# Mask phase of a four-phase transformer kernel: reordered statistics, pair eviction, row sums and low-part splits

## The reference, cut to what matters

```python
xq  = layer_norm(x, qn_w, qn_b)            # [16, 256, 512]
ctx = layer_norm(context, cn_w, cn_b)
q = (xq @ q_w).reshape(B, N, H, D)         # H = 16 heads of D = 32
kv = (ctx @ kv_w).reshape(B, M, 2, H, D)
k, v = kv[:, :, 0], kv[:, :, 1]
attn = einsum('bnhd,bmhd->bhnm', q, k) * scale
attn = where(xa_mask[:, None, :, :], neg, attn)
attn = softmax(attn, axis=-1)
out = einsum('bhnm,bmhd->bnhd', attn, v).reshape(B, N, C)
x = x + out @ proj_w + proj_b
...
```

## Time and profile before

| | |
|---|---|
| median of three runs | 2735.47 us |
| the profiled execution, its own time | 2735.95 us |
| its span, as the profile shows it | 2733.9 us |
| busy over the span | PE 96%, DVE 72%, ACT 57%, POOL 34% |
| granted TensorE clock, mean | 0.983 |

### The profile page before, as it was taken

How to read it: one execution, slowest core, us unless ns; L and a number is a source line. 1 busy time by engine, 2 the same in 40 slices (tenths; PEclk the granted TensorE clock), 3 DMA queues, 4 the chain that set the end, 5 groups by cost and what they waited for, 6 DMA issues and landing times.

```text
span 2733.9 us, 67256 instructions
## 1 busy us (share of the span) xinstructions
PE 2618.4 (96%) x23144; PEld 2244.9 (82%) x23144; DVE 1956.6 (72%) x5443; ACT 1565.1 (57%) x4742; POOL 923.0 (34%) x1097
## 2 busy tenths in 40 slices
PE   6899998998899999999999999999899999999997
PEld 5777777777688888888888888888788888888886
DVE  6888788787644344434458888888788888888887
ACT  5677767767511111111238777777667676776764
POOL 4656656655110000000002333333434343434332
PEclk8999999999999999999999999999999999999999
DMA  5666656655421101111321111111322221222210
GB/s 160 151 153 154 162 148 154 163 148 143 131 62 47 61 31 61 46 46 47 92 82 36 46 46 46 46 46 52 125 69 84 74 87 61 92 69 70 84 54 24
DMA packets 313622, 236.12 MB, mean 86 GB/s; under 512 B 150736, under 2 KB 240848, under 8 KB 312656
## 3 DMA queue, kind: packets, MB, share of 16 engines
q1 hardware_dynamic: 313552, 235.22, 30.2%
HBM read 137.65 MB, written 63.96 MB: 74 GB/s over the span
## 4 chain that ended last, share of the span: by engine, by line
PE 79%; DVE 8%; ACT 7%; issue 4%; DMA 1%; SPq 1%; POOL 0%; DVEq 0%; ACTq 0%; POOLq 0%
PE cross_work L181 16%; PE mlp_acc L3297 13%; PE mlp_f L3279 13%; PE causal_work L181 9%; PE mask_work L181 6%; PE cross_scores L2294 3%; ACT mask_prob_even L964 3%; PE cross_scores L2271 2%; PE cross_attended L2324 2%; PE causal_scores L2294 2%; PE causal_scores L2271 2%; DVE mask_scores L1555 2%; PE causal_attended L2324 1%; PE mask_scores L2271 1%; ACT mask_prob L964 1%
## 5 line engine op out<-in xcount | busy, mean ns | idle before, releaser
L3072 ACT ACTIVATE mlp_h<-mlp_f,mlp_b1col 128x512 f32<-128x512 f32 x128 | 88.3, 690 | 525.9 <-PE mlp_f L3279 525.9
L3279 PE MATMUL mlp_f<-mlp_xT_hi,mlp_w 128*128 128x512 f32 x1024 | 335.5, 389 | 0.9 <-DVE mlp_xT_lo L3165 0.9
L3179 DVE CAST mlp_hT_hi<-mlp_h 128x512 fp32r<-128x512 f32 x128 | 58.1, 454 | 370.0 <-ACT mlp_h L3072 369.8
L3297 PE MATMUL mlp_acc<-mlp_w,mlp_hT_hi 128*128 128x512 f32 x1024 | 315.2, 389 | 0.0
L964 ACT ACTIVATE cross_prob<-cross_scores,cross_low 128x256 f32<-128x256 f32 x512 | 237.5, 491 | 63.1 <-DVE cross_low L1549 63.1
L964 ACT ACTIVATE causal_prob<-causal_scores,causal_low 128x128 f32<-128x128 f32 (+1 forms) x512 | 210.6, 436 | 93.6 <-DVE causal_low L1555 93.6
L1555 DVE CUSTOM_DVE_ANT_0 mask_scores<-mask_scores,mask_mask 128x256 f32<-128x256 f32 x512 | 200.9, 454 | 47.8 <-PE mask_scores L2271 35.2
L3279 PEld LDWEIGHTS mlp_f<-mlp_xT_hi,mlp_w 128*128 128x128 f32 x1024 | 192.4, 188 | 42.0 <-DVE mlp_xT_lo L3165 1.3
L3297 PEld LDWEIGHTS mlp_acc<-mlp_w,mlp_hT_hi 128*128 128x128 f32 x1024 | 192.2, 188 | 40.0
L181 PE MATMUL causal_work<-causal_xT_hi,causal_w 128*128 128x256 f32 x1008 | 217.0, 293 | 0.3 <-DVE causal_qk_parts L1505 0.3
L3279 PE MATMUL mlp_f<-mlp_xT_lo,mlp_w 128*128 128x512 f32 x512 | 199.2, 389 | 0.0
(11 more groups left out here) (368 smaller groups left out, 8136.7 us busy)
## 6 DMA issues: line engine op xcount, KB each, us to landing
cross_x_in<-after_attention SPq DMA_DIRECT2D x17, 512.0 KB, 4.1
mask_x_in<-in_x SPq DMA_DIRECT2D x16, 512.0 KB, 4.4
mask_c_in<-in_ctx SPq DMA_DIRECT2D x16, 512.0 KB, 4.8
mask_res<-in_x SPq DMA_DIRECT2D x16, 512.0 KB, 3.8
after_attention<-mask_res SPq DMA_DIRECT2D x16, 512.0 KB, 3.1
mlp_x<-after_attention SPq DMA_DIRECT2D x8, 1024.0 KB, 5.5
mlp_stage<-in_L_xattn_fc_w SPq DMA_DIRECT2D x8, 1024.0 KB, 5.7
after_layer<-mlp_y SPq DMA_DIRECT2D x8, 1024.0 KB, 4.4
```

The source lines that it names most:

```text
L3072: act.activation(h32[:, m % 2, :], F1[m % 2][:], ACT.Gelu, bias=b1col[:, m:m + 1]).then_inc(s["gelu"], 1)
L3279: ins = pe.matmul(F1[m % 2][:], W[2 * (m // 4)][:, a, k, m % 4 * P:(m % 4 + 1) * P], xT[p][:, k, :], start=(k == 0 and n == 0), stop=(k == ...
L3297: ins = pe.matmul(ACC[t][:], hT[a][:, m % 2, t * P:(t + 1) * P], W[2 * (m // 4) + 1][:, p, m % 4, :], start=(m == 0 and n == 0), stop=(m = ...
```

## The change

Nothing is added and nothing is removed in the turns 1 to 15: every instruction is still there once, in another place of its engine's list. GpSimd's and SyncE's lists are unchanged.

```diff
@@ -1044,24 +1044,23 @@
 
             if cur and prev:
                 exps(b, 0)
+            if prev:
+                pair_kept(b, -1)
+            if not cur:
+                yield ROOM
+                post_hi(b, 1)
+                yield ROOM
+                return
+            if prev:
+                values(b, 0)
                 exps(b, 1)
-                values(b, 0)
-            if prev:
-                pair_kept(b, -1)
-            if cur and prev:
                 exps(b, 2)
+                qk(b, 1)
                 exps(b, 3)
-                qk(b, 1)
-            if cur:
-                high_halves(b, 0, 0)
-                high_halves(b, 0, 1)
-            if not cur:
-                yield ROOM
+            high_halves(b, 0, 0)
             if prev:
                 post_hi(b, 1)
-            if not cur:
-                yield ROOM
-                return
+            high_halves(b, 0, 1)
             if prev:
                 values(b, 1)
                 values_high(b)
@@ -1114,11 +1113,13 @@
             copy(b, 12)
             copy(b, 13)
             copy(b, 14)
-            post_hi(b + 1, 0)
             if not nxt:
+                post_hi(b + 1, 0)
                 yield ROOM
             copy(b, 15)
-            if not nxt:
+            if nxt:
+                post_hi(b + 1, 0)
+            else:
                 yield ROOM
 
         def causal_turn(b, prev, cur, nxt):
@@ -1730,7 +1731,8 @@
             minima(b, 2)
             if nxt and prev:
                 project(b, 0)
-            over_sums(b, 0)
+            else:
+                over_sums(b, 0)
             if not prev:
                 turn_over(b + 1, 0)
                 turn_over(b + 1, 1)
@@ -1757,6 +1760,11 @@
             if not nxt:
                 yield ROOM
                 project(b, 1)
+            if nxt and prev:
+                qk_lo(b + 1, 0)
+                mask_floats(b + 1)
+                if after:
+                    front(b + 2)
             normed(b, 0)
             if nxt and not prev:
                 turned(b + 1, 2)
@@ -1764,15 +1772,14 @@
             over_sums(b, 1)
             if not prev:
                 matrix_lo(3)
-            if nxt:
+            if nxt and not prev:
                 qk_lo(b + 1, 0)
                 mask_floats(b + 1)
-            else:
-                yield ROOM
-                yield ROOM
-            if nxt and after:
                 front(b + 2)
-            elif nxt:
+            elif not nxt:
+                yield ROOM
+                yield ROOM
+            if nxt and not after:
                 yield ROOM
 
                 dve.sem_inc(s["chain"], 2)
@@ -2468,9 +2475,11 @@
                 pe.wait_ge(s["qk_lo"], KC * b + 1)
                 queries(b, 1)
                 keys(b, 1)
+            pe.wait_ge(s["v_ready"], 2 * b + 1)
+            values(b, 1, 0)
+            if prev:
                 turn_sums(b, -1)
-            pe.wait_ge(s["v_ready"], 2 * b + 1)
-            values(b, 1, None if prev else 0)
+                values(b, 1, 1)
 
             scores(b, 1)
             pe.wait_ge(s["qk_lo"], KC * b + 2)
@@ -2507,7 +2516,8 @@
                 project(b, 1, 0)
                 if nxt:
                     project(b, 1, 1)
-            turn_sums(b, 0)
+            if not (nxt and prev):
+                turn_sums(b, 0)
 
             if not nxt:
                 yield ROOM
```

More of the change, by code:

```diff
@@ L1046, in mask_turn @@
                 exps(b, 0)
-                exps(b, 1)
-                values(b, 0)
             if prev:
                 pair_kept(b, -1)
-            if cur and prev:
-                exps(b, 2)
-                exps(b, 3)
-                qk(b, 1)
-            if cur:
-                high_halves(b, 0, 0)
-                high_halves(b, 0, 1)
             if not cur:
                 yield ROOM
+                post_hi(b, 1)
[3 more added lines that the diff above has]
+                values(b, 0)
+                exps(b, 1)
+                exps(b, 2)
+                qk(b, 1)
+                exps(b, 3)
+            high_halves(b, 0, 0)
             if prev:
                 post_hi(b, 1)
-            if not cur:
-                yield ROOM
-                return
+            high_halves(b, 0, 1)
             if prev:
@@ L1766, in mask_turn @@
                 matrix_lo(3)
-            if nxt:
+            if nxt and not prev:
                 qk_lo(b + 1, 0)
                 mask_floats(b + 1)
-            else:
+                front(b + 2)
+            elif not nxt:
                 yield ROOM
                 yield ROOM
-            if nxt and after:
-                front(b + 2)
-            elif nxt:
+            if nxt and not after:
                 yield ROOM
```

## The result

The changed kernel takes 2694.68 us, the median of four runs (2689.70 to 2697.07), against 2735.02 us for before (four runs, 2732.65 to 2736.23). The ratio is 0.9851, 95% interval 0.9834 to 0.9868: 40.3 us faster, where 55.8 were forecast. The profiled execution is the fastest of the four, 2689.70 us.

A forecast was written before the change was run, and what follows sets the result against it. TensorE's mask-phase waits, mainly on ScalarE's eviction, were the target: 36.66 + 0.25 + 0.1 + 0.2 + 0.2 - 0.3 = 37.1 us a turn against 40.94. Over 14 turns 53.8, plus 2.3: 2680, range 2663 to 2708.

The forecast's parts named there:

- blocked copies: Rival: two `over_sums` and `post_lo` on VectorE each wait for a GpSimd instruction, 1.9 us a turn on top, 2706; chance 0.20.
- a floor of 36.36: Turn without TensorE waits: 36.66 us by one form, less 0.3, half of the 0.57 by which the other form is lower.
- 0.75 of new waits: Per turn: 0.25 before `scores(b, 3)`, 0.1 for `attend` on `normed`, 0.2 on ScalarE's copies, 0.2 for the VectorE-GpSimd port.
- The long stalls and the clock: Chunks 0 and 2: waits of 2.10 and 0.94 us before row sums, plus 1.58 us of half clock in ten turns.
- Row sums behind the keys: Chunks 2 and 3: scores follow the projection at once; 0.25 us of the 0.94 wait left, 0.56 us of work moves.
- Statistics: VectorE, behind chunk 3's minima: next minima 1.75 us after `scores(b+1, 0)`, not 3.45; `attend` waiting on `normed` costs 0 to 0.1.
- Chunk 0 and ScalarE's chain: Chunk 0's 2.10 us wait goes; ScalarE's copies end 18.45 us after `scores(b, 0)`, TensorE arrives at 18.4: 0.2 us wait.
- The port, 0.2 us: VectorE's `over_sums` beside GpSimd's work: a blocked one waits at most 1.13 us, both 0 to 2.3 a turn; 0.2 taken.
- Turn 15: Has the same stall as the other turns, 2.56 us, of which 2.3 us was counted as gained.
- the floor's time of 2666: Rival: both engines' arrivals fit and nothing is blocked, 36.1 us a turn, 70 us gained, 2666; chance 0.14.
- The slower case: Rival: `attend(b+1, -2, 2)` waits for `normed` behind statistics waiting for rows of turn b+2; 2741 at 4.6 us late; chance 0.05.

The follow-up runs named there:

- the kernel before with the reduction: Kernel before, with the lift (constant added to a head's two minima) as a TENSOR_REDUCE over pairs, nothing else: 2724.38 us.
- The two remedies: Changed kernel with the lift as a TENSOR_REDUCE, 2680.70 us; or with chunk 3's queries and keys evicted one head earlier, 2680.48; both together 2667.39.
- the kernel whose TensorE shows no wait: Changed kernel with the lift as a TENSOR_REDUCE, chunk 3's queries and keys evicted one head earlier, head 0's lift directly behind its minima: 2662.14 us.
- without any lift: Constant not added to the minima in chunks 0 and 2, its instruction left out: changed kernel 2659.79 us, kernel before 2703.06 us.
- The form with 128x1: Changed kernel with the constant added by two TENSOR_SCALARs of one element per partition in place of one of two elements: 2684.56 us.

## Why the prediction was right, and where it was not

The time lies in the range and the direction is right. But 2695 is nearer to "blocked copies", 2706, than to the forecast's 2680, and the range reaches that far only for this rival, whose copies cost nothing that can be seen here: that much was luck. The 37.97 us a turn lie above the 36.5 to 37.6 that were to show the forecast. And two errors of opposite sign stand inside its 37.1 us. The forecast was a floor of 36.36 (36.66 less 0.3) and 0.75 of new waits. Measured are a floor of 35.71 and 37.97 - 35.71 = 2.26 above it.

*The long stalls and the clock:* right in that both go. The 2.10 and the 0.94 before the row sums are gone, and with them the half clock of the earlier trace rows in turns 2 to 14. But the half clock had cost far less than the 1.58 us counted for it. Chunks 0 and 1 of the kernel before, in a turn with it and in one without:

```profile
282.64:295.75 13.11, 11.01 (x122) 0.87 0.41 145
295.75:304.25 8.50, 8.50 (x78) 1.00 0.98 204
323.35:334.87 11.52, 9.42 (x121) 1.00 0.38 136
334.87:344.68 9.81, 8.99 (x77) 1.00 0.98 207
```

Together they take 21.61 us with it and 21.33 without: what chunk 0 lost, chunk 1 did not have to wait. In the kernel before with the reduction the two kinds of turn take 40.45 and 40.17 us, the same difference of 0.28. The turns of the second form were the longer ones because the lift was held in them, in chunk 2 (11.62 us, against 10.60).

*Row sums behind the keys, "0.25 us of the 0.94 as left":* this is the step that failed. 0.89 is left in nine of the turns and 0.42 in the others, plus 0.43 before the projection in the nine. I named the four `turned` on VectorE as what is late; the rows show VectorE idle for 0.62 us ahead of the low part, and ScalarE late. Its list from the minima of chunk 2 to the eviction was not laid out; only that of chunk 0 was. The two remedies bear it out from both ends. The eviction stands 8.88 us behind the chunk's scores in the long turn; with an earlier start of the exponentials (the reduction) it is 7.62, with one head fewer in front 7.98. The chunk's 1.45 us over its 8.99 without waits is the largest part of the 2.64 by which a long turn exceeds the floor.

*The floor:* busy time of a turn that stalls is not its time without stalls. By the rows, busy falls from 36.66 to 36.47, 36.11 and 35.71 as the waits go, though the work is the same. What that 0.95 us consists of was not tested; a group's row may cover short waits between its matmuls.

*Statistics:* right. The next minima start 1.96 us after `scores(b+1, 0)` (forecast 1.75, before 3.45), and `attend` waits for `normed` by 0.2 us at most in two turns. It also waits for the DMA transposes, by up to 0.36 us (and by 1.43 in turn 1, as before the change); 1.1 us of slack was forecast there, and it was less.

*Chunk 0 and ScalarE's chain:* right to a few tenths. Chunks 0 and 1 take 18.7 us in the long turn and 18.32 in the short one, forecast 18.6; 0.25 us of wait stands before the turning of chunk 1's probabilities, where I had put 0.2 one step later, before `scores(b, 2)`.

*The port, 0.2 us:* the mechanism was right, the place wrong. The copy in `over_sums` is held in the long turns (1.22 us) and `post_lo` more than before, its mean rises from 1050 to 1467 ns, and both are absorbed as far as can be seen: in the kernel whose TensorE shows no wait, that copy still takes 0.83 us and `post_lo` 1.19 to 1.41. One such copy had been held before the change too, for 1.34 us in turn 0. What cost time is the lift, which I had not looked at, since its usual row reads 0.17 us. The Trainium skill, page "SBUF — State Buffer", section "Who interferes with whom", says that a tensor_scalar in a two-port mode and an operation with two SBUF inputs share a lock with GpSimd, while tensor_reduce on this chip never contends. The trace agrees on all three: 1.44 us for the two-element TENSOR_SCALAR, 1.80 for `post_lo`, and at most 0.16 for the TENSOR_REDUCE.

*Turn 15:* 2.3 us forecast, 2.8 measured up to its last scores. The 2.56 stall is gone, but 3.08 stands in its chunk 1, where 2.28 stood.

*The rivals:* the floor's time of 2666 is what the changed kernel reaches once the lift and the eviction are mended. "Blocked copies" had the kind of hold right, and at 2706 was too slow, because the copies it named are covered. The slower case did not arise: VectorE never waited for the rows of turn b+2.

Why 40 and not 56? Not because of the hold alone: it was there before, and the change is worth 43.7 us with it gone from both kernels, 43.3 without any lift. With the lift a turn goes from 40.94 to 37.97, 2.97 us against the 3.84 forecast. In the terms of the sum, TensorE is busy 510.91 / 14 = 36.49 us a turn, 0.13 more than the 36.36, and idle for 1.48 in place of 0.75. Of the 1.48, 0.97 are the two waits in chunk 2 (9.8 and 3.8 us over 14 turns), for which 0.25 was put in; that is most of what is missing. ScalarE's chain there is as long as before: in a turn with a held lift the eviction of queries and keys stands 8.88 us behind the chunk's scores, and in the kernel before it stood 8.89 behind them (scores at 344.68 in the earlier trace rows):

```profile
353.57 0.60 ACT L942 ACTIVATE mask_qk_parts<-mask_work 128x512 fp32r<-128x512 f32 x1
```

There the wait for the pair, which is gone, had covered it. The kernel with the row sums' part alone shows the same wait of 0.42 or 0.88 us by itself.

Open is why the hold begins in four turns before and in nine after. GpSimd's last gain ends 0.30 us after the lift is issued in the long turn and 0.27 in the short one, where the lift ends with that gain. Each part alone also has it (7, 14 and 8 turns). Each count is of one execution, and how it varies between executions of one kernel was not measured.

## What to carry to other kernels

Where a loop's turns come in two forms, split each form by stage before averaging them; the second form of before already held one of the terms that decided here. When a stall goes, lay out the chain of every engine between the same two points, not only of the one that was reordered. Read the longest and not only the median time of small instructions ahead of a chain: one that usually takes 0.17 us took 1.44, and writing it as a reduction and issuing it one head sooner, with one eviction a head earlier, was worth 32.5 us on top of the change's 40.3.

## What was not expected of the hardware

- A VectorE TENSOR_SCALAR of 128x2 float32, 0.15 us by itself, took 1.41 to 1.46 us beside GpSimd's last gain and the two casts behind it, 1.17 us together: it was held over several GpSimd instructions that follow each other closely. The form with 128x1 took at most 0.155 us in 256 instances, the TENSOR_REDUCE at most 0.160 in 128.
- In the kernel before, the granted clock fell behind a stall of 2.1 us in ten of the turns 2 to 14 (to a mean of 0.65 in the earlier trace rows) and stayed at 1.00 behind the same stall in the other three. With stalls of 1.4 us in that place, in the kernel before without a lift, it stayed at 1.00 in all of them, and so it did with 1.57 to 1.88, in the kernel with the row sums' part alone. Yet with the statistics alone moved, it fell in three turns behind a shorter one: all these turns wait 1.5 us before the row sums of chunk 2, and chunk 3 behind that wait ran at 1.00 or, in three of them, at 0.83, and was 1.5 us longer then. A turn with it, its chunk 3, and a turn without:

```profile
323.43:365.41 41.98, 38.16 (x394) 0.96 0.62 159
355.42:365.41 9.99, 9.99 (x78) 0.83 0.90 217
282.97:323.43 40.46, 36.69 (x394) 1.00 0.62 159
```
